# Selected features in units of two: compares of 512 columns, and the order of selection, turning and copying that goes with them

## The reference

```python
e = jnp.stack([tbl_0[ids[:, 0]], ..., tbl_31[ids[:, 31]]], axis=1)      # 2048 x 32 x 128
z = jnp.einsum('bfd,bgd->bfg', e, e)[:, iu, ju]                          # upper triangle
h = jnp.concatenate([z, dense_ctx], axis=1)                              # 496 + 16 = 512
h = jnp.maximum(h @ W_top1 + b_top1, 0.0)                                # 512 x 512
h = jnp.maximum(h @ W_top2 + b_top2, 0.0)                                # 512 x 256
y = h @ W_top3
```

## Time and profile before

| | |
|---|---|
| Runs, median (lowest, highest) | 668.05 us (664.44, 673.72) |
| The profiled execution, its span | 667.14 us, 665.4 us |
| Busy: TensorE, its weight loads | 456.8 us (69%), 399.1 us (60%) |
| Busy: VectorE, ScalarE, GpSimd | 274.1 us (41%), 141.6 us (21%), 308.9 us (46%) |
| Mean granted TensorE clock | 0.823 of full speed |
| Compares (L562), selection matmuls (L256) | 768, 1536 |
| Gathers (L226) | 320 |
| HBM read | 41.77 MB, 63 GB/s over the span |

### The profile page before, as it was taken

The page is one execution under the profiler, slowest core; times in us unless marked ns, Lnnn a source line. Parts: engine busy times, 40 slices in busy tenths (PEclk is TensorE's granted clock), DMA queues, the critical chain, the costliest instruction groups (busy, mean ns, idle before and its releaser), DMA issues.

```text
span 665.4 us, 15716 instructions
## 1 busy us (share of the span) xinstructions
PE 456.8 (69%) x6484; PEld 399.1 (60%) x6484; DVE 274.1 (41%) x828; ACT 141.6 (21%) x268; POOL 308.9 (46%) x324
## 2 busy tenths in 40 slices
PE   2512555784598764996658856788558875489988
PEld 2411544684577653786637746677446774379967
DVE  4501663364334552235523544246432453227511
ACT  2101331031112120122111311213111222014313
POOL 6775664256632666226652566226653366420000
PEclk9855886687888877888679988788789975699999
DMA  8922823121411224012240223112131122301000
GB/s 192 255 53 74 214 78 82 27 61 51 88 38 37 67 51 90 17 40 62 56 82 24 55 55 87 32 30 68 45 87 43 43 55 49 85 24 30 5 3 2
DMA packets 32020, 42.19 MB, mean 63 GB/s; under 512 B 11796, under 2 KB 24860, under 8 KB 31992
## 3 DMA queue, kind: packets, MB, share of 16 engines
q1 hardware_dynamic: 19656, 20.64, 14.0%
q0 software_dynamic: 10240, 20.99, 12.5%
q10 hardware_dynamic: 2096, 0.17, 0.2%
HBM read 41.77 MB, written 0.01 MB: 63 GB/s over the span
## 4 chain that ended last, share of the span: by engine, by line
PE 55%; another core or an unknown queue 21%; issue 17%; DVE 4%; ACT 2%; DMA 1%; SPq 0%; ACTq 0%; DVEq 0%
PE sel_ps L256 25%; PE gram_ps L274 9%; PE mlp_ps L297 8%; PE mlp_ps L303 5%; PE rows_ps L240 5%; DVE onehot L562 3%; ACT rows_T L430 1%; PE mlp_ps L377 1%; PE mlp_ps L282 1%; DVE table_lo L585 1%; PE mlp_ps L291 1%; DMA id_rows<-ids_selected 1%; ACT rows_T L421 1%; PE mlp_ps L386 1%
## 5 line engine op out<-in xcount | busy, mean ns | idle before, releaser
L226 POOL DMA_INDIRECT gathered<-table,tile_ids x320 | 308.7, 965 | 285.7 <-PE rows_ps L240 134.2
L562 DVE TENSOR_SCALAR onehot<-id_rows,row_no 128x256 fp32r<-128x256 int32 x768 | 230.8, 372 | 261.2 <-remote 143.9
L256 PE MATMUL sel_ps<-onehot,table_hi 125*128 125x256 f32 x768 | 225.9, 323 | 99.7 <-issue 73.3
L256 PEld LDWEIGHTS sel_ps<-onehot,table_hi 125*128 125x128 f32 x768 | 167.6, 218 | 112.0 <-issue 88.5
L256 PE MATMUL sel_ps<-onehot,table_lo 125*128 125x256 f32 x768 | 215.2, 309 | 16.8 <-issue 16.5
L256 PEld LDWEIGHTS sel_ps<-onehot,table_lo 125*128 125x128 f32 x768 | 168.0, 219 | 17.0 <-issue 17.0
L430 ACT ACTIVATE rows_T<-sel_ps 128x256 f32<-128x256 f32 x96 | 59.2, 629 | 310.0 <-remote 203.6
L274 PE MATMUL gram_ps<-rows_T 128*32 128x32 f32 x4096 | 63.0, 210 | 66.5 <-ACT rows_T L430 35.9
L274 PEld LDWEIGHTS gram_ps<-rows_T 128*32 128x32 f32 x4096 | 52.0, 121 | 90.8 <-issue 48.7
L297 PE MATMUL mlp_ps<-x,w_sb 128*128 128x256 f32 x224 | 66.2, 436 | 10.6 <-issue 10.6
L240 PE MATMUL rows_ps<-ident,gathered 128*128 128x128 f32 x320 | 58.4, 302 | 12.3 <-issue 12.1
(11 more groups left out here) (23 smaller groups left out, 79.2 us busy)
## 6 DMA issues: line engine op xcount, KB each, us to landing
id_rows<-ids_selected SPq DMA_DIRECT2D x96, 128.0 KB
gathered<-table,tile_ids POOLq DMA_INDIRECT x320
pairs<-tables_selected SPq DMA_DIRECT2D x6, 448.0 KB
x<-tables_selected SPq DMA_DIRECT2D x6, 448.0 KB
w_sb<-w SPq DMA_DIRECT2D x1, 1024.0 KB
w_sb<-w SPq DMA_DIRECT2D x1, 512.0 KB
pairs<-tables_selected SPq DMA_DIRECT2D x6, 52.0 KB
x<-tables_selected SPq DMA_DIRECT2D x6, 52.0 KB
```

Of the source, the lines that this page charges most:

```text
L226: nc.gpsimd.indirect_dma_start(gathered[:, t, g, :], None, tables_gathered[g], bass.IndirectOffsetOnAxis(ap=slot_id, axis=0)).then_inc(chu ...
L256: last_op = nc.tensor.matmul(sel_ps[:, f % 2, 0, :], part[0:SEL_P, f, k, :], onehot[0:SEL_P, f % 2, k, :], start=(k == 0 and part is table ...
L562: last_op = nc.vector.tensor_scalar(onehot[:, f % 2, k, :], id_rows[:, slot, :], row_no[:, k:k + 1], None, ALU.is_equal)
```

## The change

Two selected features make a unit, 6 units in all. One compare covers both features of a unit (512 columns), and a unit's first half (4 of the 8 row groups, both features) lies in one bank of the one-hot store, its second half in the other. VectorE's half of unit u waits until the same half of unit u-1 is used. TensorE selects, per half, 8 matmuls for the first feature and 8 for the second, into one PSUM bank each; `onehot_used` rises once per half, and a new `sel_done` rises when the first feature of the unit is complete, so that ScalarE can copy it. Ids of two features come with one DMA into three slots. The stage's order becomes: chunk 0, pairs of the first tile, unit 1, chunks 1 and 2, unit 2, pairs of the second tile, chunks 3 and 4, unit 3, chunks 5 and 6, unit 4, chunk 7, unit 5, chunk 8. Unit 0 of the next pair stands where feature 0 stood; feature 1 no longer stands within the second Gram product. Ahead of the loop the same holds: two tables are split, then a unit compared and selected, then two chunks turned (units 1 to 4); the ids of a unit (from unit 2 on) are loaded ahead of its two tables.

```diff
--- before.py
+++ after.py
@@ -24,7 +24,8 @@
 PAIR = 2 * P
-ROW_SLOTS = 5
+UNITS = N_SEL // 2
+UNIT_SLOTS = 3
 RAW_SLOTS = 4
...
@@ -84,8 +85,9 @@
         gathered = sb("gathered", [P, 2, N_GATH, P])
-        onehot = sb("onehot", [P, 2, SEL_K, PAIR], F32R)
-        id_rows = sb("id_rows", [P, ROW_SLOTS, PAIR], I32)
+        onehot = sb("onehot", [P, 2, K_HALF, 2, PAIR], F32R)
+        id_rows = sb("id_rows", [P, UNIT_SLOTS, 2, PAIR], I32)
         tile_ids = sb("tile_ids", [P, n_tiles, N_GATH], I32)
...
@@ -164,16 +167,15 @@
         def _(sp):
-            def load_id_row(i, o, f):
-                slot = f % ROW_SLOTS
-                if f >= ROW_SLOTS:
-                    sp.wait_ge(onehot_ready, at(i, o, 2 * N_SEL, 2 * (f - ROW_SLOTS + 1)))
+            def load_id_rows(i, o, u):
+                slot = u % UNIT_SLOTS
+                if u >= UNIT_SLOTS:
+                    sp.wait_ge(onehot_ready, at(i, o, 2 * UNITS, 2 * (u - UNIT_SLOTS + 1)))
                 elif not known_first(i, o):
-                    before = max(g for g in range(N_SEL) if g % ROW_SLOTS == slot)
-                    sp.wait_ge(onehot_ready, at(i, o - 1, 2 * N_SEL, 2 * (before + 1)))
-                sp.dma_start(id_rows[:, slot, :],
-                             ids_selected[f:f + 1, bass.ds(at(i, o, PAIR), PAIR)].to_broadcast([P, PAIR])
+                    sp.wait_ge(onehot_ready, at(i, o - 1, 2 * UNITS, 2 * (u + UNITS - UNIT_SLOTS + 1)))
+                rows = ids_selected[2 * u:2 * u + 2, bass.ds(at(i, o, PAIR), PAIR)]
+                sp.dma_start(id_rows[:, slot, :, :], rows.unsqueeze(0).broadcast_to([P, 2, PAIR])
                              ).then_inc(id_row_in[slot], 16)
...
@@ -241,23 +242,27 @@
-            def select(i, o, f):
+            def select(i, o, u):
                 for h in range(2):
-                    pe.wait_ge(onehot_ready, at(i, o, 2 * N_SEL, 2 * f + h + 1))
-                    if h == 0 and f >= 2:
-                        pe.wait_ge(sel_moved, at(i, o, N_SEL, f - 1))
-                    elif h == 0 and not known_first(i, o):
-                        before = max(g for g in range(N_SEL) if g % 2 == f % 2)
-                        pe.wait_ge(sel_moved, at(i, o - 1, N_SEL, before + 1))
-                    for kk in range(K_HALF):
-                        k = h * K_HALF + kk
-                        for part in (table_hi, table_lo):
-                            last_op = nc.tensor.matmul(sel_ps[:, f % 2, 0, :], part[0:SEL_P, f, k, :],
-                                                       onehot[0:SEL_P, f % 2, k, :],
-                                                       start=(k == 0 and part is table_hi),
-                                                       stop=(k == SEL_K - 1 and part is table_lo))
-                    last_op.then_inc(onehot_used, 1)
+                    pe.wait_ge(onehot_ready, at(i, o, 2 * UNITS, 2 * u + h + 1))
+                    for e in range(2):
+                        if h == 0 and u >= 1:
+                            pe.wait_ge(sel_moved, at(i, o, N_SEL, 2 * u - 1 + e))
+                        elif h == 0 and not known_first(i, o):
+                            pe.wait_ge(sel_moved, at(i, o - 1, N_SEL, N_SEL - 1 + e))
+                        for kk in range(K_HALF):
+                            k = h * K_HALF + kk
+                            for part in (table_hi, table_lo):
+                                last_op = nc.tensor.matmul(sel_ps[:, e, 0, :], part[0:SEL_P, 2 * u + e, k, :],
+                                                           onehot[0:SEL_P, h, kk, e, :],
+                                                           start=(k == 0 and part is table_hi),
+                                                           stop=(k == SEL_K - 1 and part is table_lo))
+                        if e == 1:
+                            last_op.then_inc(onehot_used, 1)
+                        elif h == 1:
+                            last_op.then_inc(sel_done, 1)
@@ -308,17 +313,21 @@
                 turn_pairs(i, o - 1, 0)
+                select(i, o, 1)
+                turn(i, o, 1)
+                turn(i, o, 2)
                 select(i, o, 2)
-                turn(i, o, 1)
+                turn_pairs(i, o - 1, 1)
+                turn(i, o, 3)
+                turn(i, o, 4)
                 select(i, o, 3)
-                turn(i, o, 2)
+                turn(i, o, 5)
+                turn(i, o, 6)
                 select(i, o, 4)
-                turn_pairs(i, o - 1, 1)
-                for f in range(5, N_SEL - 1):
-                    select(i, o, f)
-                    turn(i, o, f - 2)
-                select(i, o, N_SEL - 1)
+                turn(i, o, 7)
+                select(i, o, 5)
+                turn(i, o, 8)
@@ -333,25 +342,23 @@
-            def gram1_layer2(i, o, next_pair=True):
+            def gram1_layer2(i, o):
...
                 gram_waits(i, o, 1)
-                gram_part(1, 0, 11)
+                gram_part(1, 0, 16)
                 layer2(i, o - 1, 1).then_inc(x2_done, 1)
-                gram_part(1, 11, 11)
-                if next_pair:
-                    select(i, o + 1, 1)
-                gram_part(1, 22, 10).then_inc(gram_done, 1)
...
@@ -426,9 +432,16 @@
                     act.wait_ge(gram_done, at(i, o, 2))
-                act.wait_ge(onehot_used, at(i, o, 2 * N_SEL, 2 * f + 2))
+                if f % 2 == 0:
+                    act.wait_ge(sel_done, at(i, o, UNITS, f // 2 + 1))
+                else:
+                    act.wait_ge(onehot_used, at(i, o, 2 * UNITS, f + 1))
                 nc.scalar.activation(rows_T[:, :, :, f].rearrange("p t s -> p (t s)"),
                                      sel_ps[:, f % 2, 0, :], ACT.Copy).then_inc(sel_moved, 1)
+            def move_unit(i, o, u):
+                move_selection(i, o, 2 * u)
+                move_selection(i, o, 2 * u + 1)
@@ -464,16 +477,20 @@
                 move_x0(i, o - 1, 0)
-                move_selection(i, o, 2)
+                move_unit(i, o, 1)
                 move_chunk(i, o, 1)
-                move_selection(i, o, 3)
                 move_chunk(i, o, 2)
-                move_selection(i, o, 4)
+                move_unit(i, o, 2)
                 move_x0(i, o - 1, 1)
-                for f in range(5, N_SEL - 1):
-                    move_selection(i, o, f)
-                    move_chunk(i, o, f - 2)
-                move_selection(i, o, N_SEL - 1)
+                move_chunk(i, o, 3)
+                move_chunk(i, o, 4)
+                move_unit(i, o, 3)
+                move_chunk(i, o, 5)
+                move_chunk(i, o, 6)
+                move_unit(i, o, 4)
+                move_chunk(i, o, 7)
+                move_unit(i, o, 5)
+                move_chunk(i, o, 8)
                 move_x1(i, o - 1, 0)
...
@@ -547,19 +564,17 @@
         def _(dve):
-            def compare(i, o, f):
-                slot = f % ROW_SLOTS
-                per_pair = len(range(slot, N_SEL, ROW_SLOTS))
-                dve.wait_ge(id_row_in[slot], at(i, o, 16 * per_pair, 16 * (f // ROW_SLOTS + 1)))
+            def compare(i, o, u):
+                slot = u % UNIT_SLOTS
+                dve.wait_ge(id_row_in[slot], at(i, o, 16 * UNITS // UNIT_SLOTS, 16 * (u // UNIT_SLOTS + 1)))
                 for h in range(2):
-                    if f >= 2:
-                        dve.wait_ge(onehot_used, at(i, o, 2 * N_SEL, 2 * (f - 2) + h + 1))
-                    elif not known_first(i, o):
-                        dve.wait_ge(onehot_used, at(i, o - 1, 2 * N_SEL, 2 * (N_SEL - 2 + f) + h + 1))
-                    for k in range(h * K_HALF, (h + 1) * K_HALF):
-                        last_op = nc.vector.tensor_scalar(onehot[:, f % 2, k, :], id_rows[:, slot, :],
+                    if not (known_first(i, o) and u == 0):
+                        dve.wait_ge(onehot_used, at(i, o, 2 * UNITS, 2 * u + h - 1))
+                    for kk in range(K_HALF):
+                        k = h * K_HALF + kk
+                        last_op = nc.vector.tensor_scalar(onehot[:, h, kk, :, :].rearrange("p e s -> p (e s)"),
+                                                          id_rows[:, slot, :, :].rearrange("p e s -> p (e s)"),
                                                           row_no[:, k:k + 1], None, ALU.is_equal)
@@ -590,28 +605,26 @@
                 compare(i, o + 1, 0)
+                pack_pairs(i, o, 0)
                 compare(i, o + 1, 1)
-                pack_pairs(i, o, 0)
-                compare(i, o + 1, 2)
-                compare(i, o + 1, 3)
                 pack_pairs(i, o, 1)
...
```

More of the change, by code:

```diff
@@ L69, in dlrm_tower @@
     K1, K2, K3 = w1.shape[0] // P, h1_n // P, h2_n // P
-    assert n_pairs >= 3 and (K1, K2, K3) == (4, 4, 2) and NC == 5 and N_SEL == 12 and n_pairs >= 4
+    assert n_pairs >= 3 and (K1, K2, K3) == (4, 4, 2) and NC == 5 and UNITS == 6 and n_pairs >= 4
     with ExitStack() as ctx:
@@ L128, in dlrm_tower @@
```

(41 more changed lines are left out.)

32 lines of the change are left out of this document (16 added, 16 removed).

## The result

The changed kernel took **637.73 us** (median of 4 runs, 631.05 to 645.19), the kernel before 667.03 on the same chip: ratio **0.951 [0.940, 0.963]**. The profiled execution took 645.19 us, with a span of 643.2. It was the slowest of the four and is counted as a slow one: the ratio is of the means without it, and its trace holds 22 us of the gain and not 29.

The account below looks back on a forecast made before the run. No engine fills the span; TensorE's signals, held during runs of gathers, lengthen the selection stage in six pairs. Profiled 667.14 us plus 7.4 for that stage, other terms 0 or evening out, gave 675 us, range 644 to 699.

Parts of the forecast that it names:

- TensorE's order: Feature 1's selection leaves the second Gram product and joins feature 0 ahead of it: 1.92 us moved, none saved.
- the sum: Whole-kernel total: profiled 667.14 us plus 7.4 (1.2 more a pair in the selection stage, six pairs) is 674.6.
- gathers leave TensorE's matmuls alone: On TensorE: matmuls' own durations agree with gathers not disturbing them; only the signals' arrival doesn't.
- The runs of gathers: Selection stage: first run 4 gathers instead of 8, then half the pairs at 3 runs, half at 4; 47.9 us.
- four runs in every pair: Selection stage: a case with all pairs at four runs of gathers, +15 us.
- The compares' price: VectorE: a 512-column compare taken at 0.54 us, between 0.274 and 0.548; 26.3 us a pair become 25.9, off the path.
- GpSimd's own instructions stay: GpSimd's gathers: its own instructions stay as they were; no time added for them.
- The start: Ahead of the loop: four to six features done before copies restart; -6 to +4 us, taken as 0.
- Id loads: SyncE: 12 loads a pair become 6 of twice the bytes; cost nothing, at most 7.7 us in all, doubled.
- The last pair's stage: Last pair's selection stage, no gathers beside it: stays at 23.6 to 24.2 us.
- the slower one: Selection stage: coarser steps give five runs of gathers in every pair, +29 us in all, 697 us; chance 0.34.
- Faster by count: Selection stage: each held signal costs 0.79 us, 5 fewer save 24 us in all, 644 us; chance 0.15.

Follow-up runs that it names:

- e18: Kernel before with only feature 1's selection moved ahead of the second Gram product, layer 2 five steps later; second holding chip: 657.12 us, 0.949.
- e1: Kernel before with its chunks turned in the changed kernel's order, compares, ids and signals as before; holding chip: 677.51 us, 1.016.
- e2: Changed kernel with each compare of 512 columns cut into two of 256; holding chip: 648.49 us, 0.969 to the kernel before.
- e3: Changed kernel with the ids of each feature in a DMA of their own; holding chip: 647.3 us, 0.971 to the kernel before.
- e4: Changed kernel run once more, unchanged; holding chip: 647.19 us, 0.969 to the kernel before.
- e7: Changed kernel with 12 more TensorE signals a unit to a semaphore nobody reads; free chip: 468.56 us, 1.053 to the kernel before.
- e8: Kernel before with chunks turned in twos and feature 1 selected ahead of the second Gram product; free chip: 442.51 us, 0.996.
- e12: Kernel before with only feature 1 selected ahead of the second Gram product; another free chip: 443.58 us, 1.001.
- e13: Kernel before with chunks in twos and feature 1 selected ahead of the second Gram product; third free chip: 0.995.
- e14: Kernel before with only feature 1 selected ahead of the second Gram product; third free chip: 1.000.
- e11: Kernel before with chunks in twos and feature 1 selected ahead of the second Gram product; another free chip: 440.09 us, 0.993.
- e9: Changed kernel run again, unchanged, on another free chip: 469.07 us, 1.055 to the kernel before.
- e10: Changed kernel with each 512-column compare as two of 256; another free chip: 443.67 us, 1.000 to the kernel before.

## Why the prediction was wrong

**The step that failed** is the one on TensorE's order: "1.92 us moved, none saved". I costed the moved selection by its own length and asked only who would wait for it. I did not read what stood where it left and what it would come to cover. The rows were there: chunk 9's gathers end near 283 in the middle of the second Gram product, TensorE stops there, and the clock falls. Moved ahead, the same 1.92 us are done while the gathers run. This is worth 3.0 us a pair in the profiles, 21.0 in all; the sum had 0. That it is this place is shown by e18 (place alone: the gain), by e1 (order alone: a loss), and by e2 and e3 (width and loads undone: the gain stays). Not separated are the place of layer 2, which moved with it, and the 15 us that e18 gains beyond the 21.

The prediction also held that gathers leave TensorE's matmuls alone, since their durations don't change. It looked at durations and not at starts: the stops at 281 to 284 stood in the same trace.

**The runs of gathers**: the first run of 4 came in e1 and e2, but in this kernel in pair 1 alone. With compares of 256 columns (e2) pair 2 has 4, then 16, 8 and 8, and the stage's line of the table rose by 8.1 us. That this is near the sum's 7.4 is in part luck: the line holds the first Gram product too, and four runs in every pair would have given 15. With 512 the first run has 12 gathers in five of the six pairs, and the second 16 to 24; I read this as unit 1's signal leaving before the holding begins, which isn't shown. The order alone, with features handed over singly (e1), cost 14.4 us in that line. Against before, the line stands at -1.9, +3.7 and -2.8 us in the profiles of after, e4 and e3.

**The compares' price**: 0.54 us taken, 0.40 measured from one start to the next. Four in a row, on VectorE in pair 2:

```profile
213.16 1.68 DVE L576 TENSOR_SCALAR onehot<-id_rows,row_no 128x512 fp32r<-128x512 int32 x4 [1.65 <-PE sel_ps L258]
```

The last of a row is seen whole, 0.48 us, so the three before it are 0.40 apart. Read the same way, the eight of 256 columns in 2.19 us, the last of them 0.35, are 0.263 apart and not 0.274. That makes 0.52 ns a column and 0.13 us for each instruction. "Nearly all columns" was wrong; the bounds held it. Half a unit then takes VectorE 1.7 us and not 2.2; e2, which puts the 2.2 back, has the short first run.

**"GpSimd's own instructions stay"**: in number they do, not in time. GpSimd is busy 21 us longer. On a holding chip what that costs isn't separated, but the first line of the table, 3.4 us longer in after, is back at 117.7 in e2. On a free chip it is the whole loss.

**The start**: taken at 0 within -6 to +4, measured +3.4. The first unbroken run has 76 gathers and ends at 110.4 us, where it had 44.

**Id loads**: free, as said (e3). **The last pair's stage**: 23.6 us, as said.

**The rivals**: the slower one (five runs a pair) did not come. "Faster by count" asked for 24 us in the stages, and their line fell by 1.9. e7's many signals cost nothing on a free chip; on a holding chip extra signals were not tried. "Faster by release" gave 638 us, the measured time, by another mechanism: the stage of pair 2 stayed at 46.5 us with all 32 gathers ahead of its last release. A number that fits shows no mechanism. The copies' waits had pointed me to the stage alone.

**Open**: what is late on a holding chip. It cannot be semaphores alone, since the stops at 281 to 284 stand in a row of matmuls before which the kernel has no wait. The records show neither what TensorE lacks there nor why two chips do it and three do not. The 2.6 us in the last line of the table are something else: a pause of 2.72 us in the last pair's second Gram product before (645.73 to 648.45), where nothing is gathered. The one DMA in it is a load of 16 KB of instructions, from 646.0 on. e18 has 2.03 us, with such a load from 640.5 on, and e8, e12 and e13 have 1.8 to 2.0 us on free chips; in after 0.25 us are left. That the load is the cause was not tested.

## What to carry to other kernels

When an instruction group moves, read the stretch that it leaves and the stretch that it comes to as closely as its own length: independent work put ahead of a stall can take the stall's time, and the clock may stay up with it. Cut both traces at the same instructions over the whole span before explaining a total; lists of waits named the wrong stage here. A wider VectorE instruction can slow the gathers beside it, so look at GpSimd's mean duration after each change of width.

The kernel to keep is neither of the two: feature 1's place alone (e12, e14, e18) gave 0.949 on a holding chip and 1.00 on free ones, while the whole change gave 0.951 to 0.969 on the other holding chip and 1.055 on a free one. e11's, with the order in twos, was the fastest on free chips (0.993) and gave 0.955 on a holding one.

## What the runs showed of the hardware

- The same kernel took 667 and 693 us on two chips and 444 to 445 on three. Without gathers it takes 415 to 421 on free ones. On a holding one copies and compares that wait for TensorE start again together behind runs of gathers, and TensorE stops inside rows of matmuls without a wait, 3.1 us after a run's first gather in before (281.23 and 278.15) and 5.3 in after (279.44 and 274.13). In the free ones' traces the gathers run without a gap (e9: 3.60 to 437.15 us).
- Twelve extra semaphore signals per unit from TensorE cost nothing that can be measured on a free chip (e7 468.56 against e9's 469.07, of two chips with 445.11 and 443.84 before).
- A compare costs about 0.13 us and 0.52 ns a column. At 512 columns it stretches a gather beside it from 0.96 to 1.14 us on average (e9), at 256 hardly (0.95 to 0.97, e10).
- After 2.01 us of stops, TensorE's granted clock was 0.64 over the next 3.5 us, and eight matmuls of layer 2 took 3.06 us where they take 1.92 at full clock.
